# A shorter ring, earlier table loads by SyncE and a lookup in place of idle passes, in a DLRM interaction tower on one core

## The chip, the cores and the metric

The kernel runs on one core of a Trainium2 chip. The metric is the device time of one execution in microseconds. Unchanged, three runs gave 239.93, 240.64 and 241.45 us (median 240.64). The profile is of one more execution, which took 239.78 us.

## The reference

For 512 samples, 32 embedding rows of 256 numbers each are looked up, one per table (tables of 1000, 1250 or 12500 rows). The 496 dot products of all pairs of the 32 rows and 16 dense features go through a small MLP.

```python
e = jnp.stack([tbl_0[ids[:, 0]], ..., tbl_31[ids[:, 31]]], axis=1)   # [512, 32, 256]
dots = jnp.einsum('bnd,bmd->bnm', e, e)
z = dots[:, iu, ju]                                                  # upper triangle, 496
h = jnp.concatenate([z, dense_ctx], axis=1)                          # [512, 512]
h = jnp.maximum(h @ W_top1 + b_top1, 0.0)                            # 512 -> 512
h = jnp.maximum(h @ W_top2 + b_top2, 0.0)                            # 512 -> 256
y = h @ W_top3                                                       # 256 -> 1
```

All is fp32.

## The kernel before, in words

**Tiling.** The batch is cut into 4 blocks of 128 samples. A fetch is one tile of 128 rows (4 samples by 32 fields) of 256 numbers. There are 118 fetches, 32 in block 0 and 28, 28 and 30 in the others. They are handled in 59 pairs; blocks 1, 2 and 3 begin at pairs 16, 30 and 44. 115 fetches are gathered by GpSimd (POOL) with one indirect DMA each (line 399). Three (43, 83 and 109) are fetched row by row, 320 rows by SyncE (SP) and 64 by ScalarE (ACT), with one 1 KB DMA per row (`fetch_rows`, line 366).

**The ring.** The gathered tiles go into `rows`, a ring of `RING` = 24 buffers. Before gather n, POOL waits until the fetch that had the buffer last, number n - RING in order, has been transposed (the semaphore `transposed`, which TensorE raises once per fetch). The first RING gathers wait for nothing but the ids.

**TensorE's order.** TensorE (PE) runs one list written out by hand. For each pair: four transposes of this pair's rows into `xt_ps` (`transpose_fetch`, line 417); the dot products of the pair before it (`gram_pair`, line 432), which wait for VectorE's (DVE) copy of its transposed rows (`copy_pair`, lines 334 to 345); then what tables say for this pair: steps of a lookup (`look_up`, line 468, from `LOOKUP_AT`), parts of the MLP (`mlp_at`, lines 498, 575 and 587, from `MLP_AT`), and for the last block the MLP by sets of 32 samples (`SETS_AT`, line 517 onwards). At the end of a block `gram_last` adds the dot products of the block's last 4 (or 2) groups of samples, in one go.

**Lookups.** The four hottest small tables are not gathered in blocks 1 to 3. Their rows come from a table that is held in SBUF (`hot_sb`), multiplied by a 0/1 mask which DVE makes from the ids (`make_mask`, line 675). There are 10 units (table, block) of 16 steps. Before, units 0 to 2 begin at pair 1 with 5, 5 and 6 steps in a pair, later ones take 4, 4, 4, 4 or 3, 3, 3, 3, 4. A unit may start only when ACT has copied the last one's result (line 848).

**The start.** PE runs 26 idle passes on the identity (`idle`, line 476), transposes pair 0, runs 36 more idle passes and goes on with pair 1. SP loads the row ids (`ids_sb`) and the ids of the single rows, waits for their sum from DVE and issues row DMAs. ACT waits for `ids_loaded`, loads the hot ids of block 1 (line 781), waits for the first gather, then loads table 0 in two halves (line 778). Tables 1 to 3 follow at pairs 1 to 8 (`LOAD_AT`), each half 512 KB.

**The MLP of block 1.** Its first layer stands at pairs 40 to 45 (two half parts for m = 0, 1 and whole ones for m = 2, 3), the second at 47, the third at 48. Block 2's first layer stands at 48 to 51.

```python
if n >= RING:
    pool.wait_ge(transposed, GATHERED[n - RING] + 1)
pool.indirect_dma_start(rows[:, n % RING, :], None, tables,
                        bass.IndirectOffsetOnAxis(idx[:, fetch:fetch + 1], 0)
                        ).then_inc(rows_landed[n % RING], 16)
```

Of the kernel before, what the change touches and what calls it, by code (L numbers as in the profile page):

```python
# [11 lines left out]
P = 128  # L12
# [9 lines left out]
N1 = H1 // P  # L22
# [3 lines left out]
BLOCK = 128  # L26
# [6 lines left out]
HOTS = (0, 4, 4, 2)  # L33
HOT = max(HOTS)
HOT_CHUNKS = 8
HOT_BATCH = BATCH - BLOCK
UNIT = tuple((l, b) for b in range(BLOCKS - 1) for l in range(HOT - HOTS[b + 1], HOT))
UNITS = len(UNIT)
UNIT_STEPS = HOT_CHUNKS * CHUNKS
# [7 lines left out]
FIRST_FETCH = tuple(sum(BLOCK_FETCHES[:b]) for b in range(BLOCKS))  # L47
FETCHES = sum(BLOCK_FETCHES)
PAIRS = FETCHES // 2
RING = 24  # L50

PARTS = tuple((BLOCK_GROUPS * b + first, BLOCK_GROUPS * b + end) for b in range(BLOCKS)
              for first, end in (((0, 16), (16, 32)) if b < BLOCKS - 2 else
# [26 lines left out]

GATHERED = tuple(n for n in range(FETCHES) if n not in SINGLE)

FIRST_IDLE_PASSES = (26, 36)


WIDE = H2 // QUADS
# [47 lines left out]
def mlp_stages():  # L134

    at = {}
    for n in range(2 * N1):
        at.setdefault(26 + n, []).append(("h1", 0, n // 2, n % 2, 2))
    for m in range(N2):
        at.setdefault(35 + m, []).append(("h2", 0, m))  # L140
    at.setdefault(38, []).append(("y", 0))
    for n in range(N1):
        at.setdefault(40 + n, []).append(("h1", 1, n // 2, n % 2, 2))
    for m in range(2, N1):
        at.setdefault(42 + m, []).append(("h1", 1, m, 0, 1))
    for m in range(N2):
        at.setdefault(47, []).append(("h2", 1, m))
    at.setdefault(48, []).append(("y", 1))
    for m in range(N1):
        at.setdefault(48 + m, []).append(("h1", 2, m, 0, 1))  # L150
    for m in range(N2):
        at.setdefault(53, []).append(("h2", 2, m))
    at.setdefault(54, []).append(("y", 2))
    return at
# [4 lines left out]

def lookups_by_pair():  # L160

    at = {}
    pair = 1
    for unit in range(UNITS):
        first = 0
        for steps in (5, 5, 6) if unit in (0, 1, 2, 7) else (3, 3, 3, 3, 4) if unit > 7 else (4, 4, 4, 4):
            at[pair] = (unit, first, first + steps)
            first += steps
            pair += 1
    return at  # L170


LOOKUP_AT = lookups_by_pair()
# [3 lines left out]
UNIT_START = {unit: pair for pair, (unit, first, _) in LOOKUP_AT.items() if first == 0}  # L177

TAIL_AT = 17
LOAD_AT = {TAIL_AT: ("tail",), 1: ("table", 1, 0), 2: ("table", 1, 1), 4: ("table", 2, 0), 5: ("table", 2, 1), 6: ("ids", 1),  # L180
           7: ("table", 3, 0), 8: ("table", 3, 1), 9: ("ids", 2),
           **{10 + n: ("w1_packed", n) for n in range(PACKED)}, 16: ("w2",),
           **{24 + n: ("w1", n) for n in range(SLOTS)}}

# [1 line left out]
def tower_kernel(nc, ids, single_ids, hot_ids, hot_tables, tables, dense, w1, w1_packed, w2, vectors, tail, y):  # L186
    with ExitStack() as ctx:
# [171 lines left out]
        def fetch_rows(engine, kind, lo, hi):  # L359
# [4 lines left out]
            for n, start in enumerate(starts):  # L364
                at, p = divmod(lo + n, P)
                yield engine.dma_start(single_u8[p:p + 1, at, :], tables_u8[bass.ds(start, ROW_BYTES)]  # L366
                                       ).then_inc(single_landed[at], 16)

        block = ctx.enter_context(nc.Block())

        @block.sync
        def _(sp):
            sp.dma_start(ids_sb[:], ids).then_inc(ids_loaded, 16)
            sp.dma_start(single_sb[:], single_ids).then_inc(single_loaded, 16)
            sp.wait_ge(row_at_ready, 1)
            for lo in range(0, SP_ROWS, LOAD):
                for _ in fetch_rows(sp, mybir.EngineType.SP, lo, min(lo + LOAD, SP_ROWS)):
                    pass
            sp.wait_ge(y_copied, BLOCKS + 1)
            sp.dma_start(y.rearrange("b o -> o b"), y_row[:]).then_inc(y_stored, 16)  # L380
            sp.wait_ge(y_stored, 16)
# [22 lines left out]
        def _(pe):  # L404
# [69 lines left out]
            def idle(passes):  # L474
                for _ in range(passes):
                    nc.tensor.transpose(hot_ps[:, 0, :], ident[:], ident[:])  # L476
# [121 lines left out]
                        y_all(*what)  # L598

            pe.wait_ge(ident_ready, 1)  # L600
            idle(FIRST_IDLE_PASSES[0])
            for place in range(2):
                transpose_fetch(place)
            idle(FIRST_IDLE_PASSES[1])
            for pair in range(1, PAIRS - 1):
                for place in range(2):
                    transpose_fetch(2 * pair + place)
# [43 lines left out]
        def _(dve):  # L651
# [75 lines left out]
            for pair in range(PAIRS - 1):  # L727
                if pair == 2:
                    dve.wait_ge(vec_loaded, 16)
                mlp_behind(pair)  # L730
                copy_pair(pair)
                if pair == 0:
                    make_mask(0)
                    make_mask(1)
                for unit in range(2, UNITS):
                    if pair == UNIT_START[unit] - 2:
                        make_mask(unit)
                for part, piece in DOTS_AT.get(pair, ()):
                    dots(part, piece)
                if pair == UNIT_END[UNITS - 1]:  # L740
                    dve.wait_ge(ident_ready, 1)
                    for q in range(QUADS):
                        here = slice(SET * q, SET * (q + 1))
                        nc.vector.tensor_copy(adder[here, :], ident[here, here])
                    nc.vector.tensor_copy(first_row[:], ident[:, 0:1].to_broadcast([P, SET])
                                          ).then_inc(adder_ready, 1)
# [24 lines left out]

        @block.scalar
        def _(act):
            hot_by_row = hot_tables.rearrange("l (p c) d -> l p c d", c=HOT_CHUNKS)

            def load_table(l, n):
                half = slice(n * HOT_CHUNKS // 2, (n + 1) * HOT_CHUNKS // 2)
                act.dma_start(hot_sb[:, l, half, :], hot_by_row[l, :, half, :]).then_inc(hot_loaded[l][n], 16)

            def load_ids(b):  # L780
                act.dma_start(hot_ids_sb[:, b].rearrange("p l n -> p (l n)"),
                              hot_ids[b:b + 1, :].to_broadcast([P, HOT * BLOCK])
                              ).then_inc(hot_ids_loaded[b], 16)


            act.wait_ge(ids_loaded, 16)
            load_ids(0)
            act.wait_ge(rows_landed[0], 16)
            load_table(UNIT[0][0], 0)
            load_table(UNIT[0][0], 1)  # L790
            act.dma_start(vec_sb[:], vectors).then_inc(vec_loaded, 16)
            act.wait_ge(z_zeroed, 1)
            act.dma_start(z_alone[DENSE_ALONE:DENSE_ALONE + DENSE, :], dense[0:DENSE, 0:BATCH - BLOCK]).then_inc(dense_alone_loaded, 16)
# [19 lines left out]
            def load_at(pair):  # L813
                if pair in LOAD_AT:
                    kind, *what = LOAD_AT[pair]
                    act.wait_ge(transposed, 2 * pair)
                    if kind == "table":
                        load_table(*what)
                    elif kind == "ids":
                        load_ids(*what)  # L820
                    elif kind == "w1_packed":
                        act.dma_start(w1_packed_sb[:, what[0], :], w1_packed[:, what[0], :]
                                      ).then_inc(w1_packed_loaded, 16)
                    elif kind == "w1":
                        act.dma_start(w1_sb[:, what[0], :], w1[:, what[0], :]).then_inc(w1_loaded, 16)
                    elif kind == "tail":
                        act.dma_start(tail_sb[:], tail).then_inc(tail_loaded, 16)
                    else:
                        act.dma_start(w2_sb[:], w2.rearrange("(k p) n -> p k n", p=P)).then_inc(w2_loaded, 16)
# [183 lines left out]
```

## Time and profile before

| | |
|---|---|
| median of 3 runs | 240.64 us |
| the profiled execution | 239.78 us |
| its span | 237.4 us |
| PE, PEld busy | 169.8 us (72%), 145.1 us (61%) |
| POOL, DVE, ACT busy | 110.3 (46%), 94.6 (40%), 51.0 us (21%) |
| mean granted TensorE clock | 0.892 of full |
| read by DMA | 24.70 MB |

The span runs from the first to the last instruction in the profile; 2.4 us of the execution lie outside it. PE is TensorE's matmul side and PEld its weight loads, which overlap. An fp32 matmul stands as two MATMUL and two LDWEIGHTS records, a transpose as one of each. Idle time before a group is put down to what ended it; "issue" means that nothing in the profile ended it, and "remote" that the releaser is unknown.

### The profile page before, as it was taken

To read this page: it belongs to the slowest core of one execution; us is meant where nothing else is said; L and a number is where in the kernel's file an instruction comes from. 1 tells how busy PE (TensorE), PEld (TensorE's weight loads), DVE (VectorE), ACT (ScalarE), POOL (GpSimd) and SP (SyncE) were. 2 spreads that over 40 slices of the span, in tenths; PEclk is the share of its full clock that TensorE was granted. 3 is DMA by queue.
4 is the path that set the end of the run, shared out by engine and by line. 5 is a ranking of instruction groups with operands and counts; after the bars stand their busy time and mean duration, and the time that the engine had idled before them with its cause. 6 is when DMAs were issued, how large, how long until landed. Compare 5 with 4: busy or idle time off the path is not lost.

```text
span 237.4 us, 8126 instructions
## 1 busy us (share of the span) xinstructions
PE 169.8 (72%) x3274; PEld 145.1 (61%) x3274; DVE 94.6 (40%) x308; ACT 51.0 (21%) x162; POOL 110.3 (46%) x122
## 2 busy tenths in 40 slices
PE   7821103978777777594877859969768688899976
PEld 7710002867666566583756748859646467798764
DVE  2600001214443526254254521742346417556572
ACT  0000001010132011412104320332024334425360
POOL 5777772556555565464354461556455614000000
PEclk9985555899999999769999995998999959999999
DMA  2763331557756543623235452423232312000000
GB/s 86 242 232 111 110 98 44 174 137 250 246 142 185 155 136 78 206 68 83 75 114 160 138 160 74 139 77 95 74 89 71 91 44 74 11 3 3 6 3 3
DMA packets 11349, 25.44 MB, mean 107 GB/s; under 512 B 2943, under 2 KB 4559, under 8 KB 11313
## 3 DMA queue, kind: packets, MB, share of 16 engines
q0 software_dynamic: 5520, 15.08, 21.2%
q10 hardware_dynamic: 5004, 9.40, 13.3%
q1 hardware_dynamic: 788, 0.45, 0.7%
q8 instruction: 25, 0.41, 0.7%
q14 instruction: 12, 0.09, 0.2%
HBM read 24.70 MB, written 0.00 MB: 104 GB/s over the span
## 4 chain that ended last, share of the span: by engine, by line
PE 46%; issue 20%; another core or an unknown queue 15%; DVE 6%; ACTq 6%; ACT 3%; DMA 2%; POOL 1%
PE hot_ps L468 12%; PE gram_ps L432 12%; PE xt_ps L417 7%; PE act_ps L498 4%; ACTq L366 4%; PE dve_ps L498 3%; DVE z L325 2%; DVE xt L337 2%; PE hot_ps L476 2%; PE dve_ps L575 2%; PE hot_ps L517 2%; PE act_ps L575 1%; ACT z L318 1%; ACTq L811 1%
## 5 line engine op out<-in xcount | busy, mean ns | idle before, releaser
L399 POOL DMA_INDIRECT rows<-tables,idx x115 | 109.5, 952 | 88.5 <-PE xt_ps L417 46.1
L432 PE MATMUL gram_ps<-xt 128*32 128x32 f32 x1888 | 46.3, 205 | 45.4 <-issue 44.1
L432 PEld LDWEIGHTS gram_ps<-xt 128*32 128x32 f32 x1888 | 33.3, 113 | 62.6 <-issue 59.9
L468 PE MATMUL hot_ps<-mask,hot_sb 128*128 128x128 f32 x320 | 50.7, 308 | 10.3 <-ACT hot_xt L848 6.4
L468 PEld LDWEIGHTS hot_ps<-mask,hot_sb 128*128 128x128 f32 x320 | 43.1, 210 | 12.3 <-issue 11.0
L417 PE MATMUL xt_ps<-ident,rows 128*128 128x128 f32 x228 | 38.1, 289 | 2.2 <-issue 1.4
L334 DVE COPY xt<-xt_ps 128x512 f32<-128x512 f32 x16 | 11.1, 692 | 60.4 <-remote 32.7
L345 DVE COPY last_xt<-xt_ps 128x64 f32<-128x64 f32 (+3 forms) x44 | 10.8, 245 | 58.8 <-PE xt_ps L417 42.8
L417 PEld LDWEIGHTS xt_ps<-ident,rows 128*128 128x128 f32 x228 | 28.6, 150 | 4.0 <-issue 2.4
L351 ACT COPY xt<-hot_xt 128x64 f32<-128x64 f32 (+1 forms) x43 | 10.2, 236 | 91.8 <-remote 63.2
L337 DVE COPY xt<-xt_ps 128x448 f32<-128x448 f32 (+2 forms) x43 | 26.7, 620 | 0.0
L318 ACT COPY z<-gram_ps 32x128 f32<-32x128 f32 (+1 forms) x56 | 19.4, 346 | 9.4 <-remote 8.1
L318 DVE COPY z<-gram_ps 32x128 f32<-32x128 f32 (+1 forms) x56 | 19.1, 342 | 0.9
L675 DVE TENSOR_SCALAR mask<-hot_ids_sb,hot_number 128x128 f32<-128x128 int32 x80 | 17.4, 311 | 0.0
L848 ACT COPY hot_xt<-hot_ps 128x256 f32<-128x256 f32 x10 | 6.1, 611 | 30.1 <-remote 16.0
L476 PE MATMUL hot_ps<-ident 128*128 128x128 f32 x62 | 9.0, 316 | 1.6 <-POOL ident L389 1.6
L848 ACT ACT_TABLE_LOAD x1 | 1.3, 1283 | 40.7 <-remote 40.7
L476 PEld LDWEIGHTS hot_ps<-ident 128*128 128x128 f32 x62 | 8.7, 167 | 1.6 <-POOL ident L389 1.6
L325 DVE COPY z<-gram_ps 32x64 f32<-32x64 f32 (+1 forms) x32 | 8.4, 263 | 1.2 <-PE gram_ps L432 0.8
L325 ACT COPY z<-gram_ps 32x64 f32<-32x64 f32 (+1 forms) x32 | 8.5, 267 | 1.6 <-PE gram_ps L432 1.1
L498 PE MATMUL act_ps<-z,w_packed_sb 128*128 128x128 f32 x48 | 8.9, 329 | 0.0
L498 PE MATMUL dve_ps<-z,w_packed_sb 128*128 128x128 f32 x48 | 7.9, 291 | 0.4 <-issue 0.2
(71 smaller groups left out, 89.6 us busy)
## 6 DMA issues: line engine op xcount, KB each, us to landing
single_rows<-tables SPq DMA_DIRECT2D x320, 1.0 KB
hot_sb<-hot_tables ACTq DMA_DIRECT2D x8, 512.0 KB
w_sb<-w ACTq DMA_DIRECT2D x8, 256.0 KB
rows<-tables,idx POOLq DMA_INDIRECT x115
w_packed_sb<-w_packed ACTq DMA_DIRECT2D x5, 256.0 KB
single_rows<-tables ACTq DMA_DIRECT2D x64, 1.0 KB
hot_ids_sb<-hot_ids ACTq DMA_DIRECT2D x3, 256.0 KB, 3.1
w_sb<-w ACTq DMA_DIRECT2D x1, 512.0 KB
```

What stands on the lines that cost most here:

```text
L318: last = copy(z_by_quad[FIELDS * jq:FIELDS * (jq + 1), q, first:end, :].rearrange("p g (h s) -> p g h s", s=FOURS), gram_ps[FIELDS * q:FIE ...
L325: last = copy(z_by_quad[FIELDS * jq:FIELDS * (jq + 1), q, first:end, lo:SLOTS], gram_ps[FIELDS * q:FIELDS * (q + 1), part % 3, 0:end - fir ...
L334: return copy(xt[:, bank, :, places].rearrange("p k l q f -> p (k l q f)"), xt_ps[:, bank, :, places].rearrange("p k l r -> p (k l r)"))
L337: return copy(xt[:, bank, :, places].rearrange("p k l q f -> p (k l) q f")[:, :, :, 0:COLD[b]], xt_ps[:, bank, :, places, 0:OWN[b]].rearra ...
L345: return copy(to[:, :, :, field:field + count].rearrange("p k s f -> p k f s"), ps)
L399: pool.indirect_dma_start(rows[:, n % RING, :], None, tables, bass.IndirectOffsetOnAxis(idx[:, fetch:fetch + 1], 0)).then_inc(rows_landed[ ...
L417: last = nc.tensor.transpose(xt_ps[:, fetch // 2 % 2, k, fetch % 2, :], x[:, P * k:P * (k + 1)], ident[:])
L432: last = nc.tensor.matmul(gram_ps[FIELDS * q:FIELDS * (q + 1), part % 3, at, :], x, x, start=(k == 0), stop=(k == CHUNKS - 1))
L468: last = nc.tensor.matmul(hot_ps[:, k, :], hot_sb[:, l, c, P * k:P * (k + 1)], mask[:, unit % MASKS, c, :], start=(c == 0), stop=(c == HOT ...
L476: nc.tensor.transpose(hot_ps[:, 0, :], ident[:], ident[:])
L498: last = nc.tensor.matmul(h1_ps[m], w1_packed_sb[:, s, P * m:P * (m + 1)], z[:, FOURS + s, samples] if s < FOURS else z_alone[:, samples], ...
L675: last = nc.vector.tensor_scalar(mask[:, unit % MASKS, c, :], hot_ids_sb[:, b, l, :], hot_number[:, c:c + 1], None, ALU.is_equal)
```

## The change

The ring goes from 24 to 10 buffers. SP, behind its two loads of ids, also issues the hot ids of block 1 and tables 0 and 1 (five DMAs, 2.25 MB); ACT no longer does, and no longer waits for the first gather. Tables 2 and 3 move to pairs 1, 2, 4 and 5. PE runs all 16 steps of unit 0 ahead of pair 0's transposes, and the 36 idle passes go; units 1 to 7 take 4 steps a pair from pair 1. DVE makes the masks of units 0 and 1 before it copies pair 0. Block 1's MLP stands at pairs 40 to 43, 45 and 46, its first layer in whole parts.

```diff
-RING = 24
+RING = 10
-FIRST_IDLE_PASSES = (26, 36)
+FIRST_IDLE_PASSES = 26
-    for n in range(N1):
-        at.setdefault(40 + n, []).append(("h1", 1, n // 2, n % 2, 2))
-    for m in range(2, N1):
-        at.setdefault(42 + m, []).append(("h1", 1, m, 0, 1))
+    for m in range(N1):
+        at.setdefault(40 + m, []).append(("h1", 1, m, 0, 1))
     for m in range(N2):
-        at.setdefault(47, []).append(("h2", 1, m))
-    at.setdefault(48, []).append(("y", 1))
+        at.setdefault(45, []).append(("h2", 1, m))
+    at.setdefault(46, []).append(("y", 1))
...
-    at = {}
+    at = {0: (0, 0, UNIT_STEPS)}
     pair = 1
-    for unit in range(UNITS):
+    for unit in range(1, UNITS):
         first = 0
-        for steps in (5, 5, 6) if unit in (0, 1, 2, 7) else (3, 3, 3, 3, 4) if unit > 7 else (4, 4, 4, 4):
+        for steps in (4, 4, 4, 4) if unit < UNITS - HOTS[-1] else (3, 3, 3, 3, 4):
...
-LOAD_AT = {TAIL_AT: ("tail",), 1: ("table", 1, 0), 2: ("table", 1, 1), 4: ("table", 2, 0), 5: ("table", 2, 1), 6: ("ids", 1),
-           7: ("table", 3, 0), 8: ("table", 3, 1), 9: ("ids", 2),
+FIRST_LOADS = 2
+LOAD_AT = {TAIL_AT: ("tail",), 1: ("table", 2, 0), 2: ("table", 2, 1), 4: ("table", 3, 0), 5: ("table", 3, 1),
+           6: ("ids", 1), 9: ("ids", 2),
...
             sp.dma_start(ids_sb[:], ids).then_inc(ids_loaded, 16)
             sp.dma_start(single_sb[:], single_ids).then_inc(single_loaded, 16)
+            load_ids(sp, 0)
+            for unit in range(FIRST_LOADS):
+                for n in range(2):
+                    load_table(sp, UNIT[unit][0], n)
             sp.wait_ge(row_at_ready, 1)
...
-            idle(FIRST_IDLE_PASSES[0])
+            idle(FIRST_IDLE_PASSES)
+            look_up(*LOOKUP_AT[0])
             for place in range(2):
                 transpose_fetch(place)
-            idle(FIRST_IDLE_PASSES[1])
...
-                copy_pair(pair)
                 if pair == 0:
                     make_mask(0)
                     make_mask(1)
+                copy_pair(pair)
...
             act.wait_ge(ids_loaded, 16)
-            load_ids(0)
-            act.wait_ge(rows_landed[0], 16)
-            load_table(UNIT[0][0], 0)
-            load_table(UNIT[0][0], 1)
             act.dma_start(vec_sb[:], vectors).then_inc(vec_loaded, 16)
```

## Rows read from the trace of the kernel before

**Rows 1.** The page, the span in 40 slices of 5.9 us: busy tenths and clock.
```profile
PE   7821103978777777594877859969768688899976
...
POOL 5777772556555565464354461556455614000000
PEclk9985555899999999769999995998999959999999
```

**Rows 2.** Line 399 on POOL: ns min, median, max of one; first and last start in us.
```profile
L399 POOL DMA_INDIRECT rows<-tables,idx x115: 940/946/1312, 3.3 to 198.6; - x115
```

**Rows 3.** The timeline of the start: start us, us, engine, line, operation, tile, count.
```profile
3.31 1.31 POOL L399 DMA_INDIRECT rows<-tables,idx  x1 [1.73 <-DVE idx L654]
...
6.20 22.67 SPq L366 DMA_DIRECT2D single_rows<-tables  x22
...
6.46 0.86 ACTq L778 DMA_DIRECT2D hot_sb<-hot_tables  x2
...
7.42 0.95 POOL L399 DMA_INDIRECT rows<-tables,idx  x1 [0.30 <-issue]
...
8.00 4.09 PE L476 MATMUL hot_ps<-ident 128*128 128x128 f32 x36
8.20 0.69 DVE L334 COPY xt<-xt_ps 128x512 f32<-128x512 f32 x1 [3.60 <-issue]
...
8.80 3.43 DVE L675 TENSOR_SCALAR mask<-hot_ids_sb,hot_number 128x128 f32<-128x128 int32 x16
...
13.30 0.44 PE L417 MATMUL xt_ps<-ident,rows 128*128 128x128 f32 x2 [0.99 <-issue]
```

**Rows 4.** The timeline of 34 to 43 us.
```profile
34.51 0.21 PE L432 MATMUL gram_ps<-xt 128*32 128x32 f32 x1 [2.58 <-issue]
34.98 0.95 POOL L399 DMA_INDIRECT rows<-tables,idx  x1 [0.30 <-issue]
...
40.12 0.46 PE L432 MATMUL gram_ps<-xt 128*32 128x32 f32 x14 [0.50 <-issue]
40.28 0.69 DVE L334 COPY xt<-xt_ps 128x512 f32<-128x512 f32 x1 [28.05 <-remote]
...
42.81 0.73 PE L417 MATMUL xt_ps<-ident,rows 128*128 128x128 f32 x4
```

**Rows 5.** The timeline of one pair in the middle.
```profile
46.99 0.94 POOL L399 DMA_INDIRECT rows<-tables,idx  x1 [1.03 <-PE xt_ps L417]
...
48.92 0.47 PE L432 MATMUL gram_ps<-xt 128*32 128x32 f32 x8
...
49.87 0.52 PE L432 MATMUL gram_ps<-xt 128*32 128x32 f32 x24 [0.48 <-issue]
...
50.36 0.94 POOL L399 DMA_INDIRECT rows<-tables,idx  x1 [1.17 <-PE xt_ps L417]
```

**Rows 6.** The timeline of pair 44 and the start of pair 45.
```profile
188.97 0.94 POOL L399 DMA_INDIRECT rows<-tables,idx  x1 [0.97 <-remote]
...
191.73 0.78 PE L432 MATMUL gram_ps<-last_xt 128*32 128x32 f32 x38 [0.38 <-issue]
...
192.44 2.08 PE L498 MATMUL act_ps<-z,w_packed_sb 128*128 128x128 f32 x8
...
194.74 1.06 PE L417 MATMUL xt_ps<-ident,rows 128*128 128x128 f32 x4
```

**Rows 7.** Line 399's gathers in two stretches: us, POOL busy (count), PEclk, DMA share, GB/s.
```profile
40.12:68.37 28.25, 16.41 (x18) 0.95 0.58 185
68.37:94.47 26.10, 15.02 (x16) 1.00 0.50 142
```

**Rows 8.** The timeline after the last gather: transposes of pairs 51, 52 and 54.
```profile
210.08 0.60 PE L417 MATMUL xt_ps<-ident,rows 128*128 128x128 f32 x4
...
212.22 0.60 PE L417 MATMUL xt_ps<-ident,rows 128*128 128x128 f32 x4
...
217.93 0.38 PE L417 MATMUL xt_ps<-ident,rows 128*128 128x128 f32 x2
```

More of the change, by code:

```diff
@@ L367, in fetch_rows, with load_table, load_ids @@
                                        ).then_inc(single_landed[at], 16)
+        hot_by_row = hot_tables.rearrange("l (p c) d -> l p c d", c=HOT_CHUNKS)
+        def load_table(engine, l, n):
+            half = slice(n * HOT_CHUNKS // 2, (n + 1) * HOT_CHUNKS // 2)
+            engine.dma_start(hot_sb[:, l, half, :], hot_by_row[l, :, half, :]).then_inc(hot_loaded[l][n], 16)
+        def load_ids(engine, b):
+            engine.dma_start(hot_ids_sb[:, b].rearrange("p l n -> p (l n)"),
+                             hot_ids[b:b + 1, :].to_broadcast([P, HOT * BLOCK])).then_inc(hot_ids_loaded[b], 16)
         block = ctx.enter_context(nc.Block())
@@ L773, in _ @@
         def _(act):
[L774 to L783, printed above, removed]
             act.wait_ge(ids_loaded, 16)
-            load_ids(0)
-            act.wait_ge(rows_landed[0], 16)
-            load_table(UNIT[0][0], 0)
-            load_table(UNIT[0][0], 1)
             act.dma_start(vec_sb[:], vectors).then_inc(vec_loaded, 16)
@@ L817, in load_at @@
                     if kind == "table":
-                        load_table(*what)
+                        load_table(act, *what)
                     elif kind == "ids":
-                        load_ids(*what)
+                        load_ids(act, *what)
                     elif kind == "w1_packed":
```

## The prediction

> **What bounds the kernel now.** I read the 40 slices first [rows 1]. PE is 70 to 90% busy nearly everywhere, but the five slices from 12 to 42 us show 2, 1, 1, 0 and 3 tenths, most of them at a clock of 5 tenths. POOL is at 7 tenths in four of them, and falls to 2 in the one in which PE comes back. About 26 us of the span are lost in this hole, so it is the first thing to explain.
>
> The timeline of the start and the end of the hole does so [rows 3, 4]. The first 24 gathers wait for nothing, and two more find their buffer free (pair 0 is transposed), so POOL issues 26 of them: the first at 3.31, the last at 34.98 us, 1.27 us apart. In that time PE issues one instruction each 0.7 or 1.4 us, with nothing that ends its idle time ("issue"). SP crawls too: 22 row DMAs in 22.67 us. PE's signals are late as well. Pair 1's transposes end at 13.74 us, but DVE's copy that waits for them starts at 40.28. At 40.12 all goes on at once. Divide: (40.12 - 3.31) / 26 = 1.416 us of obstruction per gather, a little more than their spacing, so that the rest piles up to 4 us after the last one.
>
> The same price stands in the middle of the kernel [rows 5]. The first of a pair's two gathers starts at 46.99. PE stops in the middle of its dot products, after 8 matmuls, and goes on at 49.87: 2.88 us after the first, 1.44 per gather. Then `transposed` gets through, and the next gathers start at 50.36, 3.37 us after the last ones. Pair 44 repeats it: gather at 188.97, PE free at 191.73, 2.76 us later [rows 6]. So through the middle a pair costs two gathers, 2.84 us, and a handover of 0.3 to 0.5 us, whatever PE has to do, as long as that is under about 2.9 us. The rows by line 399 agree: 9 pairs in 28.25 us with lookups of 5 and 6 steps, 8 pairs in 26.10 us with 4 steps, 3.14 and 3.26 us a pair [rows 7]. Only after the last of the 115 gathers, at 198.6 [rows 2], does PE's own work set the pace: pairs 51 and 52 start at 210.08 and 212.22, 2.14 us apart [rows 8].
>
> The kernel is thus three stretches: a burst in which PE gets nothing done, 1.42 us per gather; a middle at some 3.3 us a pair; and an end without gathers at PE's pace.
>
> **The ring of 10.** It moves gathers out of the burst and into the middle. Ten gathers wait for nothing. Pair 0's and pair 1's transposes can be done inside the burst, since their instructions are queued early (pair 1's were, at 13.30), and free four more. That makes 14. Pair 2's transposes stand behind 64 dot product records and a piece of lookup, which do not get through. The obstruction ends at 3.31 + 14 x 1.416 = 23.1 us instead of 40.12. Pair 2 began 2.69 us after that point [rows 4]; with one lookup step less (two matmul records of 0.2 us at this clock, 8 took 2.08 in [rows 6]) it begins 2.3 us after it, at 25.4 us instead of 42.81: **17.4 us gained**. The bounds of this term are 12 gathers (20.3 us, 20 gained) and 18 (28.8 us, 12 gained, if pairs 2 and 3 slip in).
>
> At the other end the ring takes. With 24 buffers POOL is done at pair 47; with 10 its last gather waits for fetch 106, in pair 53. Pairs 45 to 53 took 217.93 - 194.74 = 23.2 us [rows 6, 8]. Now each carries gathers. Seven of them, 45 to 51, at 3.2 us make 22.5. Pairs 52 and 53 took 5.71 together [rows 8]. They hold a set's layer 1 (128 more instructions) and block 2's layer 2, which don't pass while their three gathers obstruct (4.2 us), and half of that may be covered by what is queued: 5.7 and 2.5 more, 8.2. Sum 30.7, so **7.5 us lost**. The bounds are 2 lost (all the PE work of pairs 45 to 51 fits under 2.84 a pair, 52 and 53 as before: 25.6) and 11 (3.4 a pair, and the whole 4.2 and a handover on the last two). Five pairs of lead remain for each gather, 16 us, against 6 us at worst from issue to use in the table loads' traffic (7.42 to 13.30, [rows 3]), so the shorter ring starves nobody.
>
> **Lookup for idle passes.** 36 idle passes of 4.09 us go, between pair 0 and pair 1. They lie inside the burst and are worth nothing by themselves. The 16 steps of unit 0 are 32 matmul records: at the 36 in 4.09 us of [rows 3] 3.6 us, at the 8 in 2.08 us of [rows 6], at the lower clock, 8.3. I take 4.2. They need table 0 and mask 0, 8 of the 16 DVE instructions that took 3.43 us [rows 3], so 1.7 us. Both can be there when the 26 idle passes end, before 8 us. The lookup ends between 11 and 16 us, before the 23.1 (or 20.3) that rule. Its cover is the burst; without it, it would cost pair 0 some 4 to 8 us. The 16 steps no longer stand in pairs 1 to 3, but [rows 7] show that 5 or 6 steps or 4 cost the same, so spreading them gives 0, at most 1 us either way.
>
> **SP's loads.** Five DMAs at 0.43 us of issue (two took 0.86 on ACT) put 2.2 us in front of SP's rows, the first of which stood at 6.20 [rows 3]. Part of that time SP waited for DVE's sums. So 0 to 2.2 us for the rows, of which none is needed before pair 21: 0. 2.25 MB then compete with the first gathers. Their landing may slip to the 5.9 us of fetch 3 [rows 3], to 9.2 us for fetch 0: 1 to 3 us for pair 0, hidden behind the lookup and the burst. The rows of fetch 43 are needed some 17 us earlier than before, but SP too leaves its crawl that much earlier: 0. ACT's table loads of pairs 1 to 5 are a pair or more ahead of their use: 0. The Trainium skill ("DMA: Bandwidth & Descriptors", Issuing engines are not separate DMA queues) says that transfers of different issuers share the same 16 engines, so moving the loads to SP saves only issue time. By it this part brings nothing but the earlier start, which is the value that I take.
>
> **Block 1's MLP.** Ten matmul records stood behind pair 44's dot products on the open path: PE is at 192.44 to 194.53 with them before pair 45's transposes [rows 6]: **2.1 us gained**. The parts at pairs 40 to 43 grow from 2 or 3 to 5 steps, so by 4 to 6 records of 0.11 us each: 0 if the gathers cover them, 2.3 if not. They are nearer to the covered rows of [rows 7]: **1 us lost**. Layer 2 moves from pair 47 to 45, which counts within the 30.7.
>
> **Sum.** -17.4 + 7.5 - 2.1 + 1.0 = -11.0. From the profiled execution's 239.78 us: 228.8 us. This execution lies 0.4% under the median of the runs, so I state **228.5 us**, 5% faster. A measurement here can tell about 1% from no change.
>
> **The rivals.**
>
> *The burst is lighter than 14 gathers, or the end costs less.* Before 8 us the first gathers did not obstruct much: pair 0's signal reached DVE, whose copy starts at 8.20 [rows 3]. If obstruction needs a pile of gathers to form, ten may stay nearly free: 20 us gained at the start, and 3 us lost at the end. 239.78 - 20 - 1.1 + 3 = 221.7 us. Against it: single pairs in the middle pay the full price at once [rows 5, 6].
>
> *PE starves for its instructions, not because of the gathers* (the slower side). PE crawls over a fixed stretch of its list, some 35 to 40 instructions after the idle passes, and would crawl over as many whatever POOL does; that SP crawls in the same time speaks against it, and so do the 2.8 us of [rows 5, 6]. The crawl of 26 us then stays, behind a lookup that costs another 2 us over the idle passes, and the end still loses 7.5: 239.78 + 2 + 7.5 - 1.1 = 248.2 us. It decides as soon as the hole ends past 37 us. The Trainium skill ("Runtime: NRT & Kernel Launch", Instruction fetch mechanics) says that instructions come in 16 KiB blocks, fetched ahead and mostly hidden, which speaks against this rival.
>
> *Half of the forecast.* The obstruction ends at 23 us, but PE's queue is held by the lookup when it begins, pair 0's transposes get in only late in the burst, and a second burst of four to six gathers follows: 28 to 31 us, 10 gained. The end costs 9. 239.78 - 10 + 9 - 1.1 = 237.7 us, or 234.2 with 12 gained and the end as forecast.
>
> **How the numbers follow.** Forecast 0.55, lighter 0.22, half 0.12, instructions 0.11. The forecast's own range by its bounds is 223 to 233; to hold 8 in 10 the range takes in the lighter case and most of the half case: 219 to 237. Faster by over 1% holds the first two and most of the half case: 0.85. Within 1%: 0.05. Slower: 0.10.
>
> **What would show it.** PE's hole ends near 23 us instead of 40, with POOL's first pause after 10 to 14 gathers, and pair 2's transposes come near 25 us. The middle keeps 3.2 to 3.3 us a pair. The last gather starts at pair 53, near 205 us, and pairs 48 to 51 start about 3.2 us apart, not 2.14. The lookup of unit 0 stands between 6.5 and 16 us. It is wrong if the hole ends where it did, if pairs in the middle change their pace without a change in their gathers, or if pairs 48 to 51 stay at 2.2 us with gathers beside them.

## The result and the profile after

| | before | after |
|---|---|---|
| median (lowest to highest of 4 runs) | 240.28 us (239.31 to 241.45) | 230.70 us (230.40 to 232.33) |
| the profiled execution, its span | 239.78, 237.4 us | 230.85, 228.7 us |

The ratio is 0.9653, with an interval of 0.9602 to 0.9705: 3.5% faster, where 5% was forecast (228.5 us). The slices of the page, of 5.7 us each now, answer to [rows 1], and below them stand three groups that answer to [rows 2] and show where PE waits (out<-in, count | busy, mean ns | idle time before, what ended most of it).

```profile
PE   7674777767777694775975996967996968879876
...
POOL 5765556556555454255555354546463455551000
...
L412 POOL DMA_INDIRECT rows<-tables,idx x115 | 110.0, 956 | 96.4 <-PE xt_ps L430 54.7
L445 PE MATMUL gram_ps<-xt 128*32 128x32 f32 x1888 | 47.2, 208 | 29.8 <-issue 26.1
...
L481 PE MATMUL hot_ps<-mask,hot_sb 128*128 128x128 f32 x320 | 52.4, 314 | 12.7 <-ACT hot_xt L845 10.2
```

The hole of slices 3 to 7 is gone from PE's row, but for one slice at 4 tenths, and POOL now works up to slice 37 instead of 34. The dot products wait 26.1 us for "issue" (44.1 before). The idle time of the lookups is 12.7 us in all (10.3 before), 1.4 of it at the start, for the first mask; 10.2 are put down to ACT's copy of the last lookup (6.4 before, with 3.9 more as "issue"). So this loss is not new. In the kernel before it stands at pair 22, for one:

```profile
113.28 1.13 PE L468 MATMUL hot_ps<-mask,hot_sb 128*128 128x128 f32 x8 [3.28 <-ACT hot_xt L848]
```

The experiments come back to it.

The timeline of the start answers to [rows 3, 4]:

```profile
3.27 1.33 POOL L412 DMA_INDIRECT rows<-tables,idx  x1 [1.69 <-DVE idx L667]
...
6.65 3.30 DVE L688 TENSOR_SCALAR mask<-hot_ids_sb,hot_number 128x128 f32<-128x128 int32 x16 [2.08 <-DMA hot_ids_sb<-hot_ids]
...
8.89 1.13 PE L481 MATMUL hot_ps<-mask,hot_sb 128*128 128x128 f32 x8 [1.45 <-DVE mask L688]
...
14.73 1.04 PE L430 MATMUL xt_ps<-ident,rows 128*128 128x128 f32 x8
...
17.84 1.29 DVE L333 COPY xt<-xt_ps 128x512 f32<-128x512 f32 x2 [7.89 <-remote]
18.54 0.95 POOL L412 DMA_INDIRECT rows<-tables,idx  x1 [2.48 <-remote]
...
19.97 0.60 PE L430 MATMUL xt_ps<-ident,rows 128*128 128x128 f32 x4
...
22.29 0.94 POOL L412 DMA_INDIRECT rows<-tables,idx  x1 [0.30 <-issue]
...
24.17 0.45 PE L445 MATMUL gram_ps<-xt 128*32 128x32 f32 x17 [1.16 <-issue]
...
26.42 1.06 PE L430 MATMUL xt_ps<-ident,rows 128*128 128x128 f32 x4
```

Ten gathers, then a pause in which the signals get through (17.84: DVE's copy of a transpose that was done at 15.8), then four gathers more, and PE is let go at 24.17. Both ends fit the price of [rows 4] within 0.4 us: 3.27 + 10 x 1.416 = 17.4 and 18.54 + 4 x 1.416 = 24.2. Pair 2 gets its transposes in at 19.97, between the two crawls: the second burst of gathers has begun at 18.54, but PE runs at full pace until about 20.8.

At the other end, pairs 45 to 54 (the answer to [rows 6, 8]):

```profile
176.29 1.12 PE L430 MATMUL xt_ps<-ident,rows 128*128 128x128 f32 x4
...
182.65 1.78 ACTq L808 DMA_DIRECT2D z_alone<-z  x2
...
184.48 0.37 ACT L880 ACTIVATE h<-act_ps,vec_sb 128x128 f32<-128x128 f32 x1 [1.91 <-issue]
...
184.90 0.54 PE L600 MATMUL dve_ps<-h,vec_sb 128*1 128x128 f32 x2 [2.17 <-issue]
...
194.03 0.60 PE L430 MATMUL xt_ps<-ident,rows 128*128 128x128 f32 x4
...
197.24 0.60 PE L430 MATMUL xt_ps<-ident,rows 128*128 128x128 f32 x4
...
200.43 0.60 PE L430 MATMUL xt_ps<-ident,rows 128*128 128x128 f32 x4
...
206.33 0.66 PE L430 MATMUL xt_ps<-ident,rows 128*128 128x128 f32 x4
...
207.04 0.95 POOL L412 DMA_INDIRECT rows<-tables,idx  x1 [2.13 <-PE xt_ps L430]
...
209.30 0.38 PE L430 MATMUL xt_ps<-ident,rows 128*128 128x128 f32 x2
```

Pairs 50, 51 and 52 start 3.2 us apart, with gathers beside them, and the last gather stands in pair 53. At 184.90 PE waits for `h`: ACT's relu stands behind two DMA issues, 1.78 us together, on ACT's own queue.

To see where time went, the span is cut where PE starts the transposes of a pair (read off each kernel's timeline). The kernels are those of the experiments below. All numbers are us.

| kernel | until pair 10 | 10 to 22 | 22 to 40 | 40 to 45 | 45 to 54 | span |
|---|---|---|---|---|---|---|
| before | 68.37 | 40.64 | 65.55 | 20.18 | 23.19 | 237.4 |
| after | 49.23 | 45.33 | 63.19 | 18.54 | 33.01 | 228.7 |
| after, again | 49.18 | 44.55 | 62.89 | 18.27 | 33.05 | 227.3 |
| before, ring 10 | 49.04 | 39.46 | 64.94 | 20.28 | 30.43 | 223.6 |
| the same, again | 49.22 | 39.66 | 65.44 | 20.48 | 30.37 | 224.9 |
| before, ring 10, MLP moved | 49.64 | 40.36 | 67.03 | 18.46 | 33.46 | 228.8 |
| before, ring 10, early copy | 49.16 | 39.39 | 63.22 | 20.29 | 30.42 | 222.2 |
| after, old start | 49.59 | 40.43 | 67.40 | 18.63 | 33.39 | 228.8 |
| after, other schedule | 49.34 | 40.05 | 64.76 | 18.47 | 33.35 | 225.4 |
| after, early copy | 49.98 | 40.64 | 63.56 | 18.46 | 33.32 | 225.3 |
| after, ring 24 | 68.57 | 44.78 | 62.29 | 19.75 | 23.26 | 238.2 |
| before, MLP moved | 68.50 | 40.76 | 65.12 | 18.60 | 23.68 | 236.4 |
| after, ring 24, held back | 70.03 | 44.41 | 62.58 | 18.61 | 23.67 | 238.7 |
| before, ring 10, half of the rows | 50.00 | 39.87 | 66.30 | 20.15 | 30.88 | 227.3 |

The change gained 19.1 us until pair 10 and 1.6 from 40 to 45, and lost 2.3 from 10 to 40 (4.7 lost, 2.4 given back) and 9.8 from 45 to 54: 8.6 in all.

### The profile page after: what moved, and what is told of

It reads as the page before. It is cut to its first block, busy times and chain, and to the rows that moved or that the text cites. A ratio compares the mean times of both kernels' runs of the same rounds, so it can differ in the third digit from the quotient of the medians.

```text
span 228.7 us, 8054 instructions
## 1 busy us (share of the span) xinstructions
PE 173.2 (76%) x3238; PEld 147.1 (64%) x3238; DVE 94.5 (41%) x308; ACT 50.9 (22%) x162; POOL 110.8 (48%) x122
## 3 DMA queue, kind: packets, MB, share of 16 engines
HBM read 24.70 MB, written 0.00 MB: 108 GB/s over the span
## 4 chain that ended last, share of the span: by engine, by line
PE 39%; another core or an unknown queue 29%; issue 10%; ACTq 8%; ACT 6%; DVE 5%; DMA 2%; SPq 0%; DVEq 0%
PE gram_ps L445 10%; PE xt_ps L430 7%; PE hot_ps L481 7%; ACTq L365 5%; PE act_ps L511 3%; PE dve_ps L511 2%; DMA hot_ids_sb<-hot_ids 2%; PE hot_ps L530 2%; PE dve_ps L588 2%; ACT z L317 2%; PE act_ps L588 2%; ACT hot_xt L845 2%; DVE mask L688 1%; DVE xt L336 1%
## 5 line engine op out<-in xcount | busy, mean ns | idle before, releaser
L445 PE MATMUL gram_ps<-xt 128*32 128x32 f32 x1888 | 47.2, 208 | 29.8 <-issue 26.1
L445 PEld LDWEIGHTS gram_ps<-xt 128*32 128x32 f32 x1888 | 34.5, 115 | 47.4 <-issue 42.2
L481 PE MATMUL hot_ps<-mask,hot_sb 128*128 128x128 f32 x320 | 52.4, 314 | 12.7 <-ACT hot_xt L845 10.2
L481 PEld LDWEIGHTS hot_ps<-mask,hot_sb 128*128 128x128 f32 x320 | 44.4, 215 | 15.3 <-issue 12.1
L430 PE MATMUL xt_ps<-ident,rows 128*128 128x128 f32 x228 | 39.8, 300 | 1.2 <-issue 1.1
L350 ACT COPY xt<-hot_xt 128x64 f32<-128x64 f32 (+1 forms) x43 | 10.2, 237 | 103.6 <-remote 90.5
L430 PEld LDWEIGHTS xt_ps<-ident,rows 128*128 128x128 f32 x228 | 30.1, 156 | 2.9 <-issue 2.6
L317 DVE COPY z<-gram_ps 32x128 f32<-32x128 f32 (+1 forms) x56 | 19.1, 342 | 0.9
L530 PE MATMUL hot_ps<-w_sb,z 128*32 128x128 f32 x192 | 7.1, 274 | 0.8 <-issue 0.8
L511 PEld LDWEIGHTS act_ps<-z,w_packed_sb 128*128 128x128 f32 x48 | 7.2, 226 | 0.2
L511 PE MATMUL dve_ps<-z,w_packed_sb 128*128 128x128 f32 x48 | 7.1, 284 | 0.0
L489 PE MATMUL hot_ps<-ident 128*128 128x128 f32 x26 | 5.8, 423 | 1.6 <-POOL ident L402 1.6
```

Source lines behind the costliest of these rows:

```text
L317: last = copy(z_by_quad[FIELDS * jq:FIELDS * (jq + 1), q, first:end, :].rearrange("p g (h s) -> p g h s", s=FOURS), gram_ps[FIELDS * q:FIE ...
L430: last = nc.tensor.transpose(xt_ps[:, fetch // 2 % 2, k, fetch % 2, :], x[:, P * k:P * (k + 1)], ident[:])
L445: last = nc.tensor.matmul(gram_ps[FIELDS * q:FIELDS * (q + 1), part % 3, at, :], x, x, start=(k == 0), stop=(k == CHUNKS - 1))
L481: last = nc.tensor.matmul(hot_ps[:, k, :], hot_sb[:, l, c, P * k:P * (k + 1)], mask[:, unit % MASKS, c, :], start=(c == 0), stop=(c == HOT ...
L511: last = nc.tensor.matmul(h1_ps[m], w1_packed_sb[:, s, P * m:P * (m + 1)], z[:, FOURS + s, samples] if s < FOURS else z_alone[:, samples], ...
L530: last = nc.tensor.matmul(set_sum_ps[n][SET * m:SET * (m + 1), :], z[:, s, first:first + SET], w1_sb[:, s, P * m:P * (m + 1)], start=(s == ...
```

## The experiments

Three sets, each on a chip of its own with runs of the kernel before beside them: its median was 240.12, 243.24 and 239.67 us. Ratios are against these.

**The ring alone, in both directions.** The kernel before with 10 buffers:

```diff
-RING = 24
+RING = 10
```

> The kernel before with the ring of 10 alone. By the theory that each gather obstructs PE and SP for 1.42 us: pair 0's two signals were through before the crawl began, so 12 gathers make the first burst, and the hole ends at 3.31 + 12 x 1.416 = 20.3 us instead of 40.1. The last gather moves from pair 47 to pair 53, and pairs 45 to 53 take about 33 us as in the kernel after, instead of 23.2. Sum 240.3 - 19.8 + 9.8 = 230 us, 228 to 233. By the theory that PE starves for instructions at a fixed stretch of its list: the hole still ends near 40 us, and the time is 245 us or more.

It took 226.53 us (226.04 to 228.62), ratio 0.9502 (0.9425 to 0.9580). The timeline of its start:

```profile
17.78 0.95 POOL L399 DMA_INDIRECT rows<-tables,idx  x1 [0.30 <-issue]
...
19.22 0.21 PE L432 MATMUL gram_ps<-xt 128*32 128x32 f32 x1 [1.19 <-issue]
...
20.62 0.59 PE L432 MATMUL gram_ps<-xt 128*32 128x32 f32 x22 [1.19 <-issue]
21.06 0.95 POOL L399 DMA_INDIRECT rows<-tables,idx  x1 [2.33 <-remote]
```

Twelve gathers, and PE is free at 20.62; 12 x 1.416 us from the start of the first (3.42) gives 20.4. One number brings the whole gain, and more than the whole change does. The time is below the 228 to 233 us that were expected: pairs 45 to 53 took 30.4 us, and not the 33 of the kernel after. The kernel after with the old ring:

```diff
-RING = 10
+RING = 24
```

> The kernel after with the ring back at 24. Gather theory: 24 gathers wait for nothing and pair 0's signals come only after the burst, so PE is released at 3.27 + 24 x 1.416 = 37.3 us instead of 17.7, four more gathers follow (5.7 us), and pair 3 is transposed near 45 us instead of 26.4. The end gets its 9.8 us back. 230.7 + 18.9 - 9.8 = 240 us, 237 to 242. Instruction theory: no change in the hole, so only the end's gain: 221 us.

It took 240.93 us, ratio 1.0071 (1.0023 to 1.0118): all other edits together gain nothing with 24 buffers (by the interval they cost 0.2 to 1.2%). Its timeline:

```profile
32.51 0.95 POOL L412 DMA_INDIRECT rows<-tables,idx  x1 [0.30 <-issue]
...
37.50 1.29 DVE L333 COPY xt<-xt_ps 128x512 f32<-128x512 f32 x2 [27.75 <-remote]
38.20 0.94 POOL L412 DMA_INDIRECT rows<-tables,idx  x1 [4.74 <-remote]
...
41.95 0.95 POOL L412 DMA_INDIRECT rows<-tables,idx  x1 [0.30 <-issue]
...
43.81 0.36 PE L445 MATMUL gram_ps<-xt 128*32 128x32 f32 x9 [1.16 <-issue]
```

The hole is back with another list of instructions on PE: 24 gathers end at 37.5, four more at 43.8.

**Gathers or instructions?** To part the number of gathers from the number of buffers and from PE's list, the kernel after got 24 buffers, but POOL was held back at first as if there were 10:

```diff
-RING = 10
+RING = 24
+CAP = 10
...
+                if CAP <= n < RING:
+                    pool.wait_ge(transposed, GATHERED[n - CAP] + 1)
```

> The kernel after with 24 buffers, where POOL waits for gathers 10 to 23 as a ring of 10 does, and from the 24th on as a ring of 24. Gather theory: the start is that of the kernel after (PE released near 17.7 us, pair 3 near 26.4), but at the 25th gather some 14 buffers are free at once, so a burst of about 14 gathers comes near 45 us and a hole of about 20 us with it, in the middle of the list. Time about that of the ring of 24, 237 to 241 us. Instruction theory: no second hole, 221 us.

It took 241.59 us, ratio 1.0114 (1.0039 to 1.0189). The start is that of the kernel after (pair 3 at 26.16), but once the cap ends the 14 buffers not yet used are free at once, and with those that pairs free in the same time 17 gathers follow in one stretch, and an 18th 2.1 us after the last of them, at 59.49:

```profile
37.31 0.95 POOL L415 DMA_INDIRECT rows<-tables,idx  x1 [0.94 <-PE xt_ps L433]
...
39.34 0.26 PE L448 MATMUL gram_ps<-xt 128*32 128x32 f32 x3 [0.25 <-issue]
...
57.36 0.94 POOL L415 DMA_INDIRECT rows<-tables,idx  x1 [0.30 <-issue]
...
59.26 0.69 DVE L334 COPY xt<-xt_ps 128x512 f32<-128x512 f32 x1 [21.45 <-remote]
...
62.75 1.84 PE L484 MATMUL hot_ps<-mask,hot_sb 128*128 128x128 f32 x7 [0.84 <-issue]
...
64.39 1.06 PE L433 MATMUL xt_ps<-ident,rows 128*128 128x128 f32 x4
```

Pair 7 starts at 38.27, pair 8 at 64.39. PE crawls at a place of its list that it passes at full pace in every other kernel (pair 7 takes 3.3 to 3.6 us there), and for as long as the gathers give: 37.31 + 18 x 1.416 = 62.8, and PE goes on at 62.75. The part of the burst that was held back came at 37 us, and its price came with it. The rival "PE starves for its instructions" falls, and "the burst is lighter" too: the loss is per gather wherever they stand.

**Per gather or per row?** The kernel before with 10 buffers, where each gather fetches 64 rows. The upper 64 rows of each buffer stay zero, so half of the gathered data is left out of the computation:

```diff
-                pool.indirect_dma_start(rows[:, n % RING, :], None, tables,
-                                        bass.IndirectOffsetOnAxis(idx[:, fetch:fetch + 1], 0)
+                pool.indirect_dma_start(rows[0:64, n % RING, :], None, tables,
+                                        bass.IndirectOffsetOnAxis(idx[0:64, fetch:fetch + 1], 0)
...
+            nc.vector.memset(rows[64:P, :, :], 0.0).then_inc(rows_set, 1)
```

> The kernel before with the ring of 10, where each gather fetches 64 rows and not 128; rows 64 to 127 of every gathered tile stay zero, set once by DVE at the start (2.7 us more there). If the obstruction is the work of a gather's rows, it halves to about 0.7 us a gather, PE sets the pace at 2.2 to 2.6 us a pair and the time is 185 to 200 us. If it is a fixed cost of each gather, 1.42 us and 3.3 us a pair remain, 225 to 230 us.

It took 227.45 us, ratio 0.9496 (0.9430 to 0.9561), against 0.9542 (0.9492 to 0.9592) with 128 rows in the same set: half of the rows is worth nothing that can be measured. The gathers' group, then the timeline:

```profile
L400 POOL DMA_INDIRECT rows<-tables,idx x115: 901/905/1252, 4.0 to 204.9; - x115
```

```profile
17.75 0.90 POOL L400 DMA_INDIRECT rows<-tables,idx  x1 [0.31 <-issue]
...
21.05 0.58 PE L418 MATMUL xt_ps<-ident,rows 128*128 128x128 f32 x2 [1.73 <-issue]
...
41.96 0.90 POOL L400 DMA_INDIRECT rows<-tables,idx  x1 [1.21 <-PE xt_ps L418]
...
45.23 0.91 POOL L400 DMA_INDIRECT rows<-tables,idx  x1 [1.14 <-PE xt_ps L418]
```

The page shows that the edit does what it says: 17.17 MB are read by DMA instead of 24.70. One gather takes 905 ns of POOL instead of 946, and the hole is (21.05 - 4.0) / 12 = 1.42 us per gather, as before. A pair in the middle still takes 3.27 us. The memset brings pair 0 from 6.6 to 9.2 us, which the burst hides. The obstruction does not shrink with the rows, nor with the bytes: between 64 and 128 rows it is a fixed cost of the gather.

**Block 1's MLP alone**, with both rings:

```diff
-    for n in range(N1):
-        at.setdefault(40 + n, []).append(("h1", 1, n // 2, n % 2, 2))
-    for m in range(2, N1):
-        at.setdefault(42 + m, []).append(("h1", 1, m, 0, 1))
+    for m in range(N1):
+        at.setdefault(40 + m, []).append(("h1", 1, m, 0, 1))
     for m in range(N2):
-        at.setdefault(47, []).append(("h2", 1, m))
-    at.setdefault(48, []).append(("y", 1))
+        at.setdefault(45, []).append(("h2", 1, m))
+    at.setdefault(46, []).append(("y", 1))
```

> The kernel before with block 1's MLP at pairs 40 to 43, 45 and 46 alone. From the two traces: 2.9 us less at pair 44, 1.3 us more at pairs 40 to 43, the second layer moved within pairs that PE itself paces, 0. Sum 1 to 2 us faster, 238.5 to 239.5 us. If that part brought nothing, 240.3.

With 24 buffers: 238.83 us, ratio 0.9959 (0.9915 to 1.0003).

> The kernel before with the ring of 10 and block 1's MLP moved: the change without SP's loads and without the lookup at pair 0. The ring alone gave 226.5 us, the whole change 230.7. If the ring and the MLP are all that helps and their gains add up, 226.5 less 1 to 2 us: 225 us. If the 4 us that the whole change lacks come from the MLP beside the gathers, 229 us or more.

With 10 buffers: 231.78 us, ratio 0.9547 (0.9419 to 0.9674), too wide to tell from the ring alone. The table can tell. With 24 buffers the move gains 1.6 us from pair 40 to 45 and loses 0.5 from 45 to 54, 1.1 us net, the sum that the prediction gave. With 10 buffers, in which gathers run beside these pairs, it gains 1.7 to 2.2 from 40 to 45, but from 45 to 54 every kernel with the move took 33.0 to 33.5 us, and every one with the MLP in its old place 30.4 (30.9 with half of the rows): 2.6 to 3.1 lost. The cause shows in two timelines, first of the kernel before with 10 buffers (second run):

```profile
181.10 1.80 ACTq L811 DMA_DIRECT2D z_alone<-z  x2
...
185.56 0.81 PE L587 MATMUL dve_ps<-h,vec_sb 128*1 128x128 f32 x4
```

and of the same with the MLP moved:

```profile
181.70 1.80 ACTq L809 DMA_DIRECT2D z_alone<-z  x2
183.54 0.37 ACT L881 ACTIVATE h<-act_ps,vec_sb 128x128 f32<-128x128 f32 x1 [1.93 <-issue]
...
183.96 0.58 PE L585 MATMUL dve_ps<-h,vec_sb 128*1 128x128 f32 x2 [3.86 <-ACT h L881]
```

Behind pair 48, `y` finds its relu done. Behind pair 46 it comes before ACT has issued the two moves that stand ahead of the relu, and PE waits 3.86 us (2.17 in the kernel after). Pair 46 then takes 6.1 us to pair 47 (3.9 in the kernel after) instead of 0.9. The wait is shown; that it makes up all of the 2.6 to 3.1 us is the likely reading, not tested by itself.

**The start, the schedule and the copies.** The kernel after with the old idle passes, the old lookup schedule and the old order on DVE, but with the new loads on SP:

```diff
-FIRST_IDLE_PASSES = 26
+FIRST_IDLE_PASSES = (26, 36)
...
-    at = {0: (0, 0, UNIT_STEPS)}
+    at = {}
...
-    for unit in range(1, UNITS):
+    for unit in range(UNITS):
...
-        for steps in (4, 4, 4, 4) if unit < UNITS - HOTS[-1] else (3, 3, 3, 3, 4):
+        for steps in (5, 5, 6) if unit in (0, 1, 2, 7) else (3, 3, 3, 3, 4) if unit > 7 else (4, 4, 4, 4):
...
```

> The kernel after with the start and the lookup schedule of before (36 idle passes, units 0 to 2 from pair 1 with 5, 5 and 6 steps a pair, masks behind pair 0's copy), but ring, SP's loads and MLP as changed. Theory A, the schedule costs: with it as before, waits for ACT's copy at the change of unit move back from pairs 17, 21, 25 to 18, 22, 26, where they overlap with gathers, and the time is 225 to 227 us. Theory B, SP's early loads cost: it stays near 230 us.

231.51 us, ratio 0.9577 (0.9495 to 0.9660). The kernel after with units 3 and 7 in other numbers of pairs, so that from pair 13 on the units end in the same pairs as before:

```diff
-        for steps in (4, 4, 4, 4) if unit < UNITS - HOTS[-1] else (3, 3, 3, 3, 4):
+        for steps in (5, 5, 6) if unit == 7 else (3, 3, 3, 3, 4) if unit == 3 or unit > 7 else (4, 4, 4, 4):
```

> The kernel after with unit 3's lookup in five pairs (3, 3, 3, 3, 4) and unit 7's in three (5, 5, 6), so that all changes of unit from pair 13 on stand at the pairs of before; lookup of unit 0 still ahead of pair 0. Theory A, the place of the changes of unit costs: 226 to 227 us. If it is the lookup ahead of pair 0 that costs, 230 us.

230.23 us, ratio 0.9536 (0.9443 to 0.9628). And the kernel after in which ACT copies a finished lookup in the same pair, right behind its placing copies and ahead of its dot products, moves and loads, instead of in the next pair:

```diff
+                place(pair + 1)
                 for unit in range(UNITS):
-                    if UNIT_END[unit] == pair - 1:
+                    if UNIT_END[unit] == pair:
                         copy_looked_up(unit)
-                place(pair + 1)
```

> The kernel after, where ACT copies a finished lookup in the same pair, right behind its placing of the hot rows, instead of in the next one behind the moves and row DMAs. The waits for the copy at the changes of unit are 2.0, 3.5, 1.6, 1.6 and 1.5 us in the trace of after. If they cost what they show, up to 10 us go, of which gathers then fill some: 223 to 227 us. If the gathers only take their place, 230 us.

228.30 us, ratio 0.9449 (0.9365 to 0.9534). On this chip (where the kernel before took 243.24 us) the intervals of all four kernels with 10 buffers overlap, so the ratios settle nothing between them, and neither the old start nor the other schedule reached the 225 to 227 us expected for the case that the new schedule is what costs. The pieces of the span look clearer than they are. From pair 10 to 22 these three kernels take 40.1 to 40.6 us, and those with the new schedule and the late copy 44.4 to 45.3. But part of that is where the table is cut: in the new schedule PE changes units at pairs 17, 21 and 25, in the old one at 18, 22 and 26, so that one costly pair more falls into the piece. From pair 10 to 40 the new schedule took 107.0 to 108.5 us, the old one 104.4 to 107.8 (the highest is the kernel after with the old start), the other schedule 104.8 and the early copy 104.2. The mean granted clock in that stretch differs too: 0.92 in the kernel after, 0.95 with the old start, 1.00 with the other schedule. So it is not shown that the new places of the changes cost something.

What the traces do show is what a change of unit costs. The timeline of the kernel after, between pair 21 at 86.92 and pair 22 at 94.56:

```profile
90.08 1.04 ACTq L808 DMA_DIRECT2D z_alone<-z  x1
...
91.22 0.75 ACTq L365 DMA_DIRECT2D single_rows<-tables  x2
92.01 0.61 ACT L845 COPY hot_xt<-hot_ps 128x256 f32<-128x256 f32 x1 [2.02 <-issue]
...
92.76 2.00 PE L481 MATMUL hot_ps<-mask,hot_sb 128*128 128x128 f32 x8 [3.45 <-ACT hot_xt L845]
...
95.46 0.95 POOL L412 DMA_INDIRECT rows<-tables,idx  x1 [5.23 <-PE xt_ps L430]
```

PE may not start the next unit's lookup before ACT has copied the last. ACT stands behind its own DMA issues, so PE waits 3.45 us, pair 22's transposes are late, and POOL has nothing to do for 5.23 us. With the ring alone (second run) the same wait stands at pair 22 with 3.26 us, and POOL's with 3.84. With the early copy the three pairs with a change take 12.5 us together, in the kernel after as with the ring alone (12.6), instead of 18.2 to 18.8 and 15.9 to 17.0. Over the six pairs 17, 18, 21, 22, 25 and 26, which hold the changes of both schedules, it is 27.5 and 27.7 us in the kernel after against 26.2 and 27.1 with the ring alone, so most of that difference is where the changes stand.

**The ring with the early copy.** The last set asked whether the ring alone is better than the whole change, and whether the copy helps there. First the two again:

> The kernel before with the ring of 10 alone, a second time, beside the kernel after on one chip. The first time its ratio to the kernel before was 0.950, that of the kernel after 0.965, on other chips. If the lookup at pair 0, its schedule, SP's loads and the MLP together cost something: it is 1 to 4 us faster than a_again. If the difference was the chips': both within 1 us.

228.25 us (226.72 to 228.94), ratio 0.9542 (0.9492 to 0.9592).

> The kernel after, unchanged, on the chip of the ring of 10 alone. 0.965 of the kernel before again if its figure holds; 0.95 if the first measurement was the chip's.

230.81 us (229.49 to 232.96), ratio 0.9668 (0.9613 to 0.9723). The intervals are apart: lookup, loads, schedule and MLP together cost 2.6 us over the ring alone. By the pieces of these two traces, 4.9 are lost from 10 to 22, 2.6 given back from 22 to 40, 2.2 gained from 40 to 45 and 2.7 lost from 45 to 54: 2.8. Then the kernel before with the two edits:

```diff
-RING = 24
+RING = 10
...
+                place(pair + 1)
                 for unit in range(UNITS):
-                    if UNIT_END[unit] == pair - 1:
+                    if UNIT_END[unit] == pair:
                         copy_looked_up(unit)
-                place(pair + 1)
```

> The kernel before with the ring of 10 and ACT's copy of a finished lookup in the same pair. In a_early the waits at the changes of unit fell from 1.4 to 3.4 us to 0.5 to 0.7 us and the time was 0.945 of the kernel before. Here the waits sum to 9.1 us. If half of them comes through, 0.935, and it is the fastest so far; if gathers fill them, 0.950 as without.

224.47 us (223.14 to 224.74), ratio 0.9375 (0.9330 to 0.9421): the fastest of all, 1.7% under the ring alone and 2.7% under the kernel after, on the same chip. One change of units, in the kernel before with 10 buffers:

```profile
78.47 0.61 ACT L848 COPY hot_xt<-hot_ps 128x256 f32<-128x256 f32 x1
...
79.22 1.13 PE L468 MATMUL hot_ps<-mask,hot_sb 128*128 128x128 f32 x8 [1.54 <-ACT hot_xt L848]
```

and with the early copy:

```profile
77.47 0.61 ACT L848 COPY hot_xt<-hot_ps 128x256 f32<-128x256 f32 x1
...
78.22 1.20 PE L468 MATMUL hot_ps<-mask,hot_sb 128*128 128x128 f32 x8 [0.55 <-issue]
```

Over all units the lookups' idle time falls from 10.7 us to 5.6, as their groups in the two pages have it, of which 9.1 had been put down to ACT's copy.

## Why the prediction was right, and where its sizes were off

**The bound.** That a gather costs PE 1.42 us is borne out for bursts of 4 and 10, 12, 18 and 24 gathers in four kernels, and with half of the rows. It carried the sign and nearly all of the size.

**The ring's start, -17.4.** Measured -18.7 at pair 3 and -19.1 at pair 10. The 14 gathers came as said and let PE go at 24.2 instead of 23.1. What was off is that pair 2's transposes stand behind records "which do not get through": they went in at 19.97, between the crawls of ten gathers and of four that the prediction did not see, so pair 3 stood at 26.4. The two misses pull in opposite ways, so it is partly luck that the term came out within 2 us. The second burst is the one that the rival "half of the forecast" told of; it came, but with four gathers and at once, so it cost nothing beyond the 14.

**The middle, 0.** Measured +2.3 from pair 10 to 40, and +2.3 again between the kernel after and the ring alone on one chip. The prediction said "[rows 7] show that 5 or 6 steps or 4 cost the same, so spreading them gives 0, at most 1 us either way", and that a pair costs 3.2 to 3.3 us whatever PE has to do. What it left out are the changes of unit. There PE waits 1.5 to 3.5 us for ACT's copy, which stands behind whatever DMAs ACT issues in those pairs, and the pair takes 5 to 8 us. The mean pair from 10 to 40 took 3.54 us before and 3.62 after. This loss was in the page of before, as 10.3 us of the lookups' idle time, 6.4 of it under ACT's name, and was not read.

How the +2.3 came about stays open. The three waits are nearly as long before (1.54, 3.28 and 1.54 us) as after (1.90, 3.45 and 1.52). The kernel with the old start and schedule took 107.8 us in this stretch, as long as those with the new schedule. And three kernels with 10 buffers that are the same up to pair 40 took 104.4, 105.1 and 107.4 us on three chips, so a spread as large as the term is there without any edit.

**Pairs 40 to 43, +1.0, and pair 44, -2.1.** Measured +1.3 (13.04 us instead of 11.76) and -2.9 (5.50 instead of 8.42).

**The tail, +7.5.** Measured +9.8: 33.0 us where 30.7 was said. The ring alone takes 30.4, so the sum for the gathers held, by parts that were off both ways (21.6 us where 22.5 was said, and 8.9 on the last two where 8.2 was). What was mis-sized is "Layer 2 moves from pair 47 to 45, which counts within the 30.7": it costs 2.6 to 3.1 us where gathers run, and 0.1 to 0.5 in the kernels with 24 buffers, where they don't. With it the MLP's move is no gain of 1.1 us but a loss of 0.5 to 1.3 in the kernels with 10 buffers (51.3 to 52.0 us from pair 40 to 54 instead of 50.7 to 50.9, half of the rows left aside).

**The lookup in the burst, 0; SP's loads, 0.** The lookup stood from 8.89 to 14.89 us, within the 6.5 to 16 of the prediction, and ended before the burst did. That it needed nothing from the tables later than the masks shows in its first row, which waits for DVE, and DVE for the hot ids. Pair 10 stands at the same time with all of this (49.2 us) and with the ring alone (49.0 and 49.2), so both were hidden, as said. No run took SP's loads away by themselves.

**Sum.** -19.1 + 2.3 + 1.3 - 2.9 + 9.8 = -8.6, where -11.0 was said. The 2.4 us of difference are +2.3 in the middle and +2.3 in the tail, less 1.7 at the start and 0.5 net for pairs 40 to 44. In both of the first two stretches, work that PE waits for stands behind DMA issues in ACT's queue. In the middle the early copy shows what that costs, but it costs it before as well as after, so it does not explain the +2.3. In the tail only the wait itself is shown. The total lies near the forecast because the start carries it; the other terms are off by up to 2.3 us each.

## What to carry to other kernels

Prefetching deeper is not free where the fetch itself obstructs the engine that is the bound: count the gathers that may run before the first piece of work is done, and multiply by what one costs that engine. (No ring other than 10 and 24 was run here, so 10 need not be the best.) When work is moved within a schedule, look not only at how much stands in each step but at which steps hold the handovers, and what the other engine has queued ahead of its side of each. A DMA issue on an engine that also evacuates results costs its time (0.4 to 1.0 us in the rows above) to whoever waits behind it.

## What the hardware did that was not expected

- A gather by POOL holds back TensorE's instructions and its signals for 1.42 us, longer than POOL is busy with it (0.946 us) or the spacing of a burst (1.25 to 1.27 us), so a burst of 24 is still felt some 4 us after its last one has ended (33.5 and 37.5 us). With 64 rows instead of 128 the 1.42 us are the same. In a burst PE gets one instruction in each 0.7 or 1.4 us (its matmuls at 17.82, 19.22 and 20.62 us with 10 buffers). The crawl does not set in with the first gather: in the kernel before PE ran on until 13.9 us, 10 us into the burst, and in the later bursts for about 2 us (from 18.54 to 20.8, from 37.31 to 39.1). What it is that they share is open; no run here tells it.
- TensorE's finished work is announced late as well: in the kernel after with 24 buffers, DVE was idle for 27.75 us before it got the signal of transposes that were done by 16 us.
- Fewer buffers were faster, by 5%, though each gather is issued 14 fetches later.
